# Expert gates in DRAM rows of their own, an earlier start of the statistics, and a new order of ScalarE's and TensorE's steps ahead of the expert tiles

## What is computed

```python
h = (x - mean) * rsqrt(var + 1e-5) * ln_g + ln_b              # over D = 256; x is 8 x 512 x 256
h_norm = (h - h.mean(1)) * rsqrt(h.var(1) + 1e-8)             # over the 512 positions
sty = relu(hyp @ sty_w1 + sty_b1) @ sty_w2 + sty_b2           # hyp: small network on the subject's embedding
gamma, beta = split(sty);  gamma = softplus(gamma) + 1e-8
h = h_norm * gamma + beta
gates, idx = top_k(softmax(h_flat @ router_w), 2);  gates /= gates.sum(-1)
hid = relu(h_flat @ exp_w1[e] + exp_b1[e])                    # 8 experts, 256 -> 1024
eout = hid @ exp_w2[e] + exp_b2[e]                            # 1024 -> 256
out = x + sum over the two chosen experts of gate * eout      # N = 4096 tokens
```

## Time and profile before

| | us |
|---|---|
| median of three runs | 495.33 |
| lowest and highest | 493.65 and 496.61 |
| the profiled execution | 495.07 |
| its span | 493.1 |
| TensorE busy | 453.9 (92%) |
| VectorE busy | 383.5 (78%) |
| ScalarE busy | 278.0 (56%) |
| GpSimd busy | 225.0 (46%) |

### The profile page before, as it was taken

One profiled execution on the slowest core, in us unless ns is written; L12 is line 12 of the kernel. 1 busy time (PEld: TensorE's weight loads), 2 busy tenths in 40 slices (PEclk: granted clock), 3 DMA queues, 4 the chain that ended last, 5 costly groups with the idle time before them and its releaser, 6 DMA issues.

```text
span 493.1 us, 15848 instructions
## 1 busy us (share of the span) xinstructions
PE 453.9 (92%) x5696; PEld 414.9 (84%) x5696; DVE 383.5 (78%) x1440; ACT 278.0 (56%) x840; POOL 225.0 (46%) x183
## 2 busy tenths in 40 slices
PE   7958748999999999999999999999999999999990
PEld 5744437899999899999999999999899999999990
DVE  4988858899888878878888888888888877777640
ACT  2558526566665666655566565566566555555440
POOL 0850121444554554555555454554555544444422
PEclk9689979999999999999999999999999999999996
DMA  8952673444444434434444443444443332322321
GB/s 317 414 178 86 170 237 119 88 99 109 89 88 94 93 87 99 110 87 90 92 94 92 115 90 89 94 92 97 104 96 88 48 54 47 56 45 47 49 30 22
DMA packets 37820, 51.68 MB, mean 105 GB/s; under 512 B 8064, under 2 KB 29840, under 8 KB 37488
## 3 DMA queue, kind: packets, MB, share of 16 engines
q0 software_dynamic: 13632, 18.91, 22.4%
q1 hardware_dynamic: 21488, 31.14, 19.8%
q10 hardware_dynamic: 2624, 0.62, 0.5%
HBM read 36.74 MB, written 18.11 MB: 111 GB/s over the span
## 4 chain that ended last, share of the span: by engine, by line
PE 79%; DVE 7%; DMA 5%; ACT 3%; issue 2%; POOL 1%; SPq 1%; ACTq 0%; DVEq 0%; POOLq 0%
PE bank L700 37%; PE bank L707 35%; PE bank L655 3%; DMA out_rows<-yout,tok 2%; PE bank L649 2%; DVE bns L773 1%; DMA par<-in_params 1%; DMA h_rows<-wlo 1%; PE bank L519 1%; PE bank L531 1%; DVE tns L797 1%; DVE wlo L1160 1%; ACT hid L465 1%; DVE hidlo L1175 1%; DMA hg<-h_rows,tok 1%
## 5 line engine op out<-in xcount | busy, mean ns | idle before, releaser
L465 ACT ACTIVATE hid<-bank,par 128x128 f32<-128x128 f32 x568 | 162.8, 369 | 163.8 <-PE bank L700 161.0
L700 PE MATMUL bank<-hThi,whi 128*128 128x128 f16 x1136 | 188.9, 220 | 5.4 <-issue 1.7
L700 PE MATMUL bank<-hTlo,whi 128*128 128x128 f16 x1136 | 188.8, 220 | 0.0
L330 POOL DMA_INDIRECT out_rows<-yout,tok x71 | 122.3, 1722 | 111.3 <-ACT yout L477 91.5
L700 PE MATMUL bank<-hThi,wlo 128*128 128x128 f16 x1136 | 156.8, 220 | 0.0
L707 PE MATMUL bank<-wlo,hidhi 128*128 (+1 forms) x568 | 154.8, 273 | 0.0
L707 PE MATMUL bank<-whi,hidlo 128*128 (+1 forms) x568 | 154.8, 273 | 0.0
L707 PE MATMUL bank<-whi,hidhi 128*128 (+1 forms) x568 | 154.8, 273 | 0.0
L322 POOL DMA_INDIRECT hg<-h_rows,tok x71 | 83.1, 1170 | 113.2 <-DVE tok L1151 92.4
L700 PEld LDWEIGHTS bank<-hThi,whi 128*128 (+1 forms) x1136 | 111.2, 98 | 15.2 <-issue 7.1
L700 PEld LDWEIGHTS bank<-hTlo,whi 128*128 (+1 forms) x1136 | 111.6, 98 | 5.5
(11 more groups left out here) (171 smaller groups left out, 444.0 us busy)
## 6 DMA issues: line engine op xcount, KB each, us to landing
stage<-in_exp_w SPq DMA_DIRECT2D x64, 256.0 KB, 3.0
whi<-in_x SPq DMA_DIRECT2D x8, 512.0 KB, 8.4
out_rows<-in_x SPq DMA_DIRECT2D x8, 512.0 KB, 15.8
h_rows<-wlo SPq DMA_DIRECT2D x8, 512.0 KB, 4.0
hg<-h_rows,tok POOLq DMA_INDIRECT x71
out_rows<-yout,tok POOLq DMA_INDIRECT x71
b2row<-in_exp_b SPq DMA_DIRECT2D x1, 1024.0 KB, 20.4
par<-in_params SPq DMA_DIRECT2D x1, 517.5 KB, 6.2
```

Source lines behind the costliest of these rows:

```text
L330: gp.indirect_dma_start(out=out, out_offset=bass.IndirectOffsetOnAxis(ap=tok[:, t:t + 1], axis=0), in_=yout[:, t % 2, :], in_offset=None, ...
L465: ins = S(hid32[:, par, c * P:(c + 1) * P], bk_hid[half][:, (c - 4 * half) * P:(c - 4 * half + 1) * P], ACT.Relu, bias=vcol[:, bass.ds(e * ...
L700: hid_ins = MM(o, lhs[w, k], h[:, par, k * P:(k + 1) * P], start=(n == 0), stop=(n == 3 * KD - 1))
```

## The change

The rows of h and the gates get DRAM tensors of their own (`h_rows` with 256 numbers to a row, `gate_rows` with 8). A sequence of h is stored in pieces of four whole rows, 4 KB; all gates are stored by one transfer, which ScalarE issues. GpSimd gathers a tile's gates into `gt` with an indirect transfer of their own, a second one for each tile beside the one for the rows. Row gathers start on the stores of h alone. VectorE's statistics begin ahead of everything that needs the parameters or the subjects. On ScalarE square roots and modulations stand ahead of row copies; TensorE's list follows that order, and `back` alternates banks from the third sequence on. VectorE's router works through the first part before it starts the second. Chunks 4 and 5 are converted ahead of tile 0, chunks 6 and 7 in tile 0. TensorE has twelve more warming products ahead of tile 0.

```diff
-    h_dram = nc.dram_tensor("h_rows", (ROWS, HROW), F32).ap()
+    h_dram = nc.dram_tensor("h_rows", (ROWS, D), F32).ap()
+    g_dram = nc.dram_tensor("gate_rows", (ROWS, E), F32).ap()
...
         def bk_back(i):
-            return banks[5] if i >= BP * 2 and i % 2 == 1 else banks[7]
+            return banks[5] if i >= BP and i % 2 == 1 else banks[7]
...
         def chunks_of(t):
             if t < 3:
-                return range(4 + 2 * t, 6 + 2 * t)
+                return ((6, 7), (), (8, 9))[t]
             return range(7 + t, min(8 + t, CHUNKS))
...
                 sp_.wait_ge(s_hrow, 2 * b + 2)
-                sp_.dma_start(h_v[b], hrow[b].rearrange("p (j d) -> p j d", j=JB)).then_inc(s_hst, 16)
+                sp_.dma_start(h_v[b], hrow[b]).then_inc(s_hst, 16)
 
-            for b in range(6):
-                store_h(b)
-            sp_.wait_ge(s_comb, 1)
-            for b in range(BP):
-                store_gates(sp_, b)
-            for b in range(6, B):
+            for b in range(B):
                 store_h(b)
...
+            sp_.wait_ge(s_gh[0], 16)
             for i in range(4, 8):
-                if i % 2 == 0:
-                    sp_.wait_ge(s_gh[i // 2 - 2], 16)
                 load_chunk(i)
...
+            def gather_gates(t):
+                gp.wait_ge(s_tok, t + 1)
+                if t >= NHG:
+                    gp.wait_ge(s_gate, t - NHG + 1)
+                gp.indirect_dma_start(out=gt[:, t % NHG, :], out_offset=None, in_=g_dram,
+                                      in_offset=bass.IndirectOffsetOnAxis(ap=tok[:, t:t + 1], axis=0)).then_inc(s_gg[t % NHG], 16)
...
+            gp.wait_ge(s_spare, 16 * 6)
             gp.wait_ge(s_hst, 16 * B)
-            gp.wait_ge(s_spare, 16 * 4)
-            gp.wait_ge(s_combst, 16 * B)
             for t in range(3):
                 gather(t)
+            gp.wait_ge(s_combst, 16)
+            for t in range(2):
+                gather_gates(t)
             gp.wait_ge(s_init, 16 * B)
             for t in range(TILES + 2):
                 if t >= 2:
                     scatter(t - 2)
+                if t + 2 < TILES:
+                    gather_gates(t + 2)
                 if t + 3 < TILES:
                     gather(t + 3)
...
             act.wait_ge(s_comb, 2)
-            for b in range(BP, B):
-                store_gates(act, b)
+            act.dma_start(comb_v, comb.rearrange("p (b n) -> p b n", b=B)).then_inc(s_combst, 16)
...
             tile_hi(0, 0)
+            for i in range(4, 6):
+                w_hi(i)
...
             warm(6, 1)
+            warm(12, 1)
             tile_transpose(0)
...
             def gate(t, e):
-                V.tensor_copy(gates[:, t:t + 1], hg[:, t % NHG, bass.ds(e + D, 1)]).then_inc(s_gate, 1)
+                ve.wait_ge(s_gg[t % NHG], 16 * (t // NHG + 1))
+                V.tensor_copy(gates[:, t:t + 1], gt[:, t % NHG, bass.ds(e, 1)]).then_inc(s_gate, 1)
...
             at = lookup(1, at)
             slot_steps(3, 1)
             first = expert_numbers(ve, nei[0:1, 2, 0:1])
+            at = lookup(2, at)
+            slot_steps(4, 0)
             w_lo(0)
             w_lo(1)
-            at = lookup(2, at)
             tile_lo(0, 0)
-            w_lo(2)
-            w_lo(3)
-            slot_steps(4, 0)
+            for i in range(2, 6):
+                w_lo(i)
```

158 lines of the change are left out of this document (74 added, 84 removed).

## The result

The changed kernel takes 498.28 us (median of 20 runs, 497.0 to 499.43), the kernel before in the same comparison 495.58 us (20 runs, 493.65 to 498.7). The ratio is 1.0041, with a 95% interval from 1.0021 to 1.006. So the change costs 2.0 us by the ratio and 2.7 us by the medians; forecast was a gain of 3.1 us to 492.2, and the range ended at 495.0. By the ratio the size is under half a per cent, but the sign is wrong and the time outside the range.

What follows compares the result with a forecast made beforehand. TensorE's matmuls bound the loop, so only an earlier loop start could win: 2.05 (first gather) + 0.15 + 0.8 (first tiles) = 3.0 us, 495.2 to 492.2 us; range 489.8 to 495.0, own range 491.1 to 493.4.

Steps and rivals of the forecast that it cites:

- cost nothing: Steady loop: GpSimd's added gate gather, about 1.2 us a tile, fits beside matmuls of 5.63 us; no loss.
- 3.04 + 3.3 + 1.05: First relu behind gather(0): loads issued on its landing, their flight, conversions of chunks 4 and 5; given as 7.45 us.
- the tile part: First tiles: slot steps end at R (first relu) + 10.5, tile 3's rows land at R + 10.0; summed as 0.8 us.
- The front: Start to modulate(2): earlier statistics bring hB 1.9 us earlier and modulate(2) to about 33.45 instead of 34.99.
- The rival by which small steps under the normalisation lengthen: Front: four VectorE steps under GpSimd's normalisation lengthen by SBUF contention; result about 1 us later, 493.2; no chance given.
- To the router: time_deviation(3) 2.7 us earlier, spent waiting for router_exp(0) at 52.0; selection at 57.05, 1.7 us later.
- To the first gather: Store of h issued at 59.8, flight 3.9 us, landed at 63.7; gather(0) at 64.55, 2.05 us earlier.
- the other input, the first tokens ... doesn't bind: Ahead of gather(0): tokens follow the selection by 6.8 us, at 63.85, and don't hold the gather.
- The first tiles: From gather(0) to the loop: first product near 69.8, first relu at 72.0 instead of 74.19, 2.2 us earlier.
- lands near 72.4, 0.7 ahead of the split that stands behind it; I take nothing: First tiles: gates(0), issued as fourth gather, named a possible loss but costed at zero.
- Steady tiles: Main loop: tiles stay at TensorE's 5.63 us, with room on GpSimd for the gate gather; no cost.
- The rival of GpSimd as the bound: Loop: three indirect transfers a tile make GpSimd slower than TensorE, 499 at 2.0 us per gate gather; 0.07 with other steady losses.

Runs made afterwards that it cites:

- e14: e13 with 36 more warming products in three TensorE waits (10 ahead of sequence 3's transposes, 18 and 8 around the second row transposes): 495.10 us.
- e7: e3 with VectorE's steps in the two halves of the router mixed as in the kernel before: 496.14 us.
- e13: e7 with router_exp(1) on ScalarE behind two row copies of the first exponential instead of six: 495.43 us.
- e1: The changed kernel with the gates of tiles 0 and 1 gathered between the row gathers instead of behind all three: 497.47 us.
- e3: The changed kernel with both the edit of e1 and the edit of e2: 496.13 us.
- e4: The changed kernel with gates again in one row with h, gathered together, with eight gate stores: 496.86 us, ratio to the kernel before 1.0021.
- e6: The kernel before with only the gates put in rows of their own, stored by one transfer and gathered apart: 497.76 us, ratio 1.0037.
- e15: e14 with 4 added gathers of gate rows that nobody reads: 493.12 us, ratio to the kernel before 0.9922.
- e2: The changed kernel with chunks 4 and 5 converted behind the first relu and VectorE's rests behind the first split, as before: 498.17 us.

## Why the prediction was wrong

Two steps failed: the added gate gathers, which "cost nothing", made GpSimd's drain at the end 2.65 us longer, and the gates of tile 0, for which I took nothing, landed 3.2 us later than forecast. The smaller misses stand with them, in order of time. Two slips in the sum change nothing: 3.04 + 3.3 + 1.05 is 7.39 and not 7.45, and the tile part is worked out as 0.9 and added as 0.8.

**The front** was right: hB 1.77 us earlier (forecast 1.9), modulate(2) at 33.32 (33.45). The rival by which small steps under the normalisation lengthen came true in part: of the four steps ahead of modulate(2), those that write hA and hB took 0.38 and 0.41 us instead of 0.16 each, the other two did not change, and the four together took 0.4 us more, not 1. time_deviation(3) came 1.0 us behind the forecast (42.42 against 41.45), and copy_logits(0) with it. The step that missed is the transposes of sequences 5 and 6 on TensorE:

```profile
31.73 1.09 PE L566 MATMUL bank<-cst,whi 128*128 128x128 f32 x4 [3.21 <-ACT wlo L414]
34.24 3.65 PE L527 MATMUL bank<-cst,whi 128*128 128x128 f32 x16 [1.42 <-ACT whi L410]
37.82 2.22 PE L539 MATMUL bank<-whi,par 128*32 128x512 f32 x16
39.97 1.09 PE L527 MATMUL bank<-cst,whi 128*128 128x128 f32 x8
```

Sixteen of them took 3.65 us at a clock of 0.50, behind waits of 3.21 and 1.42 us, which came from moving row copies and their transposes back; with those waits filled (e14) they took 2.57 us at 1.00. And the first logits (L539), which the prediction has out of the way, still ended just as the last transposes began.

**To the router**: forecast 52.0, measured 52.30, and largest(1) at 53.45 (53.1). The gain was spent there as foreseen, but that the number fits is partly luck: the chain from copy_logits(0) started 1.0 us late (42.99 against 42.0) and took 9.3 us instead of 10.0. The second half then took 4.29 us to the end of the selection where 3.95 was worked out. The selection was to be 1.7 us later and was 2.4. I held VectorE's order for the cause; e7 and e13 show that ScalarE's second exponential, which the change puts 4.2 us behind the first instead of 2.2 (behind six row copies instead of three), binds nearly as long. I had not costed that move at all.

**To the first gather**: the last row copy ended at 60.41 (59.75), and the store flew 2.8 us where I took 3.9. The Trainium skill (DMA: Bandwidth & Descriptors, § Anatomy of one DMA) gave an estimate of 3.2 us for the flight; the eight stores took 2.6 to 3.3, so it was nearer than mine. (The Trainium skill gives that fit for transfers of the software path, issued by GpSimd. These were issued by SyncE, and in other kernels here the longest of them took 4.5.) But the flight no longer mattered: "the other input, the first tokens ... doesn't bind" was false. They were written at 64.27, and the gather began 0.9 us later, at 65.17. A gain of 1.43 us instead of 2.05. It was false by the prediction's own numbers, too: tokens at 63.85 come 0.15 us behind a store landed at 63.7, and with them as the bound a shorter flight couldn't have given the 491.5 worked out for it.

**The first tiles** hold the first large error. I wrote of gates(0) "lands near 72.4, 0.7 ahead of the split that stands behind it; I take nothing". It landed at 75.62. I took it for a transfer like any other (the median of all gate gathers is 2.4 us), but it was issued as four weight loads of 256 KB went out, and flew 6.39 us. These also took 4.0 us, not 3.3, so the relu came at 73.78 and not at 72.0. Behind both, TensorE was idle for 3.5 us and came back at the lower clock. From the first relu to the entry it took 21.36 us, and 20.25 before; in e1, where only the wait for the gates is gone, 20.24. So the late gates cost 1.1 us, and the gain of 0.8 that the sum has for this part wasn't there at all; why not is open. Of 3.7 us between forecast and measured at the entry of the loop, 0.6 went in the gather, 1.2 in the weights, 1.1 in the gates and 0.8 in that term; with both waits removed (e3) the entry is at 92.79, 1.65 us earlier than before. The thin margin of 0.7 us should have had a price, with the longest flight in the range.

**Steady tiles** were right: from the second scatter to the last it took 389.61 us, and 389.42 before, and GpSimd kept its idle time (busy 247.26 of 383.08 us). Row gathers even became shorter, 0.995 us against 1.197. The rival of GpSimd as the bound didn't occur.

**The end** is the largest error, and it was in no term of the sum: 2.65 us of GpSimd's drain. I wrote of the added gathers "cost nothing, cover the matmuls". That holds for the loop and not for what follows it. e4 and e6 show that it comes and goes with the gates' gathers, e15 that it counts in full. Without it the change would have been near zero: by subtraction e3 would be near 493.5, the changed kernel near 495.6.

How large the loss looks rests also on the kernel before: its own median moved between 495.39 and 497.06 in four groups, with the share of executions at a lower mean clock (13 of 35, 16 of 34, 12 of 31 and 17 of 33 were under 0.965). The sign doesn't: the changed kernel's 498.28 is above all four.

**Open**: what sets the drain's length; and whether the 6.39 us of gates(0) come from the weight loads or from standing fourth, behind three row gathers, on its queue. In e1, issued second, the gates were no longer late, but they were also issued 1.8 us ahead of the four loads (68.04 against 69.86). That the place alone does it is made unlikely by gather(1) of e13, which stood third and flew 5.66 us beside the loads.

## What to carry to other kernels

Look at what lies between the last scatter and the end of the span when the number of GpSimd's indirect transfers changes; here it was between 0.6 us less and 2.65 us more, and only a measurement told its sign. When one wait is late, list everything that ends within two microseconds of it: removing one of two such waits gave 0.1 us (e2) or 0.8 (e1), removing both 2.15 (e3). And a chain that is moved on one engine has to be followed for its second half too: an exponential three copies later held nearly as long as the order that it was blamed on.

## What was unexpected of the hardware

GpSimd's final drain took 3.697, 4.317, 5.003, 5.452, 5.461, 5.493 or 6.963 us, with the indirect transfers that GpSimd had issued, the same each time for the same number of each kind, and shorter with 217 transfers than with 213. For the same work behind the same waits TensorE was granted 1.00 in one execution and 0.50 in another between 36 and 42 us (the kernel before and e6), 3.8 us of difference at time_deviation(3); over 133 executions of the kernel before, mean granted clock and time have a correlation of -0.94.
